# A graph attention layer on one core: TensorE copies the queries of four tiles to PSUM with identity products, VectorE multiplies and sums them there

## What is computed

```python
Q = (jnp.einsum('nc,rch->rnh', x, Wq) + bq[:, None, :]).reshape(R, N, HEADS, OUT)
K, V = ...                                   # the same with Wk, bk and Wv, bv
q_i = Q[edge_type, dst]
k_j = K[edge_type, src]
v_j = V[edge_type, src]
score = jnp.sum(q_i * k_j, axis=-1) * scale
seg = dst * R + edge_type
m = jax.ops.segment_max(score, seg, num_segments=N * R)
e = jnp.exp(score - m[seg])
s = jax.ops.segment_sum(e, seg, num_segments=N * R)
alpha = e / s[seg]
out = jax.ops.segment_sum(v_j * alpha[..., None], dst, num_segments=N)
x = _layernorm(x + out.reshape(N, HD) + bias, axis=-1)
```

## Time and profile before

| | us |
|---|---|
| median of three timed runs (lowest, highest) | 3232.29 (3231.82, 3235.07) |
| the profiled execution, its own time | 3212.14 |
| its span, first to last instruction | 3210.3 |
| busy: PE / VectorE / ScalarE / POOL | 1759.5 / 1668.4 / 1012.9 / 1763.2 |

### The profile page before, as it was taken

One profiled execution on the slowest core, in us unless ns is written; L12 is line 12 of the kernel. 1 busy time (PEld: TensorE's weight loads), 2 busy tenths in 40 slices (PEclk: granted clock), 3 DMA queues, 4 the chain that ended last, 5 costly groups with the idle time before them and its releaser, 6 DMA issues.

```text
span 3210.3 us, 25454 instructions
## 1 busy us (share of the span) xinstructions
PE 1759.5 (55%) x6003; PEld 1152.3 (36%) x6003; DVE 1668.4 (52%) x3077; ACT 1012.9 (32%) x3902; POOL 1763.2 (55%) x1794
## 2 busy tenths in 40 slices
PE   7999833333699952443444444444444444444479
PEld 3444311111244422343433333434433433333455
DVE  8884100000244346565656665656666656566666
ACT  2233200000000002444544454445445444444541
POOL 1004577666100027676777767777777777676435
PEclk9999955555899985566656656666666566656665
DMA  5335776676434457555656555655555565565413
GB/s 177 108 120 190 253 228 215 204 219 207 164 147 159 152 197 226 175 172 174 177 171 178 176 172 169 176 175 174 176 168 174 173 177 174 167 180 169 130 45 103
DMA packets 285615, 553.24 MB, mean 172 GB/s; under 512 B 43605, under 2 KB 167719, under 8 KB 285466
## 3 DMA queue, kind: packets, MB, share of 16 engines
q0 software_dynamic: 106496, 327.26, 35.2%
q1 hardware_dynamic: 142836, 156.41, 14.8%
q10 hardware_dynamic: 36134, 67.94, 5.8%
HBM read 397.78 MB, written 153.65 MB: 172 GB/s over the span
## 4 chain that ended last, share of the span: by engine, by line
PE 30%; another core or an unknown queue 23%; issue 17%; DVE 17%; ACT 10%; POOL 2%; DVEq 1%; DMA 1%; SPq 0%; ACTq 0%; POOLq 0%
PE sums L549 15%; ACT region L768 9%; PE sums L610 8%; DVE acc L1025 5%; DVE region L963 3%; POOL region L378 2%; DVE region L831 2%; PE sums L653 2%; PE sums L651 2%; DVE region L1012 2%; DVE region L965 2%; DVE region L942 1%; PE sums L546 1%; PE bank L570 1%
## 5 line engine op out<-in xcount | busy, mean ns | idle before, releaser
L610 PE MATMUL sums<-region 128*128 128x130 f32 x3328 | 754.2, 408 | 964.9 <-DVE region L1029 460.8
L378 POOL DMA_INDIRECT region<-kv_tab,kvidx x832 | 854.7, 1027 | 752.3 <-DVE region L956 352.7
L610 PEld LDWEIGHTS sums<-region 128*128 128x128 f32 x3328 | 692.8, 311 | 1017.2 <-issue 725.6
L549 PE MATMUL sums<-region,acc 128*128 128x512 f32 (+2 forms) x1568 | 759.7, 631 | 307.7 <-issue 174.3
L768 ACT ACTIVATE region<-region 128x64 f32<-128x64 f32 x3328 | 835.1, 334 | 102.1 <-issue 97.8
L1025 DVE TENSOR_TENSOR acc<-acc,sums 128x256 f32 x832 | 348.2, 419 | 544.3 <-remote 352.7
L361 POOL DMA_INDIRECT region<-q_tab,qidx x391 | 372.8, 953 | 438.1 <-DVE qidx L867 253.6
L549 PEld LDWEIGHTS sums<-region,acc 128*128 128x128 f32 (+1 forms) x1568 | 304.1, 205 | 687.5 <-issue 517.7
L942 DVE TENSOR_TENSOR region<-sums,region 128x512 f32<-128x512 f32 (+1 forms) x245 | 168.8, 691 | 698.8 <-remote 312.6
L383 POOL DMA_INDIRECT region<-q_tab,qidx x441 | 454.7, 1031 | 134.6 <-issue 134.6
L748 ACT COPY region<-bank 128x128 f32<-128x128 f32 x26 | 6.9, 266 | 1316.9 <-issue 988.2
(11 more groups left out here) (175 smaller groups left out, 873.1 us busy)
## 6 DMA issues: line engine op xcount, KB each, us to landing
kv_tab<-region ACTq DMA_DIRECT2D x48, 1280.0 KB
q_pre<-region SPq DMA_DIRECT2D x391, 128.0 KB
region<-q_pre SPq DMA_DIRECT2D x391, 128.0 KB
q_tab<-region SPq DMA_DIRECT2D x48, 640.0 KB
region<-q_tab,qidx POOLq DMA_INDIRECT x832
region<-kv_tab,kvidx POOLq DMA_INDIRECT x832
region<-in_x SPq DMA_DIRECT2D x96, 128.0 KB, 2.2
out<-region SPq DMA_DIRECT2D x48, 128.0 KB, 1.7
```

The costliest lines, as they stand in the source:

```text
L378: pool.indirect_dma_start(ring[:, s % KS, i, :], None, kv_tab, bass.IndirectOffsetOnAxis(ap=kvidx[:, t:t + 1], axis=0)).then_inc(s_got[s % ...
L549: done = nc.tensor.matmul(bank[o % 4][0:n, 0:w], acc[:, k, t * P:t * P + n], w_sb[:, k, :, :].rearrange("p u c -> p (u c)")[:, c0:c0 + w], ...
L610: done = nc.tensor.matmul(bank[i][:, h * W:(h + 1) * W], ring[:, q % KS, i, h * P:(h + 1) * P], oneh[:, q % 2, i, :], start=True, stop=True)
```

## The change

In each pass TensorE first runs a new function, `lift(s)`. It waits for the gathered rows of step s, its query rows and the scores of the step before, and multiplies the 128x1024 queries by the identity in two products of 128x512, which puts a copy in PSUM banks 4 and 5 (now one tensor, `pairs`). It raises a new semaphore, s_lift. VectorE waits for that one and for the gathered rows, multiplies the keys in SBUF with the queries in PSUM, writes over them in PSUM, and reduces from there. POOL and SP wait for s_lift where they waited for s_sc before they refill a slot of `qring`.

```diff
         bank = [sums[:, i, :] for i in range(4)]
-        bank += [ctx.enter_context(nc.psum_tensor(f"bank{i}", [P, 512], f32)) for i in range(4, 8)]
+        pairs = ctx.enter_context(nc.psum_tensor("pairs", [P, 2, 512], f32))
+        bank += [pairs[:, i, :] for i in range(2)]
+        bank += [ctx.enter_context(nc.psum_tensor(f"bank{i}", [P, 512], f32)) for i in (6, 7)]
+
+        qk = pairs.rearrange("p b (i w) -> p (b i) w", w=C)
...
                 if s >= QS:
-                    pool.wait_ge(s_sc, s - QS + 1)
+                    pool.wait_ge(s_lift, s - QS + 1)
...
                 if s >= QS:
-                    sp.wait_ge(s_sc, s - QS + 1)
+                    sp.wait_ge(s_lift, s - QS + 1)
...
+            def lift(s):
+
+                pe.wait_ge(s_got[s % KS], gathered(s))
+                pe.wait_ge(s_gotq[s % QS], 16 * sum(AHEAD[s % QS:s + 1:QS]))
+                if s > 0:
+                    pe.wait_ge(s_sc, s)
+                for half in range(2):
+                    done = nc.tensor.matmul(bank[4 + half][:, 0:2 * C], ident[:],
+                                            qring[:, s % QS, 2 * half:2 * half + 2, :].rearrange("p i c -> p (i c)"),
+                                            start=True, stop=True)
+                done.then_inc(s_lift, 1)
+
             pe.wait_ge(s_ready, 1)
             for s in range(NSB + LAG):
                 q = s - LAG + 1
+                if s < NSB:
+                    lift(s)
                 weights_a(s)
...
             def scores(s):
                 dve.wait_ge(s_got[s % KS], gathered(s))
-                dve.wait_ge(s_gotq[s % QS], 16 * sum(AHEAD[s % QS:s + 1:QS]))
-                q = qring[:, s % QS, :, :]
-                c(nc.vector.tensor_tensor(q, ring[:, s % KS, :, 0:C], q, ALU.mult))
+                dve.wait_ge(s_lift, s + 1)
+                c(nc.vector.tensor_tensor(qk, ring[:, s % KS, :, 0:C], qk, ALU.mult))
                 g = SB * (s % PERC)
                 nc.vector.tensor_reduce(sc[:, (s // PERC) % 2, :, g:g + SB].rearrange("p h g -> p g h"),
-                                        q.rearrange("p i (h d) -> p i h d", h=H), AX.X, ALU.add).then_inc(s_sc, 1)
+                                        qk.rearrange("p i (h d) -> p i h d", h=H), AX.X, ALU.add).then_inc(s_sc, 1)
```

More of the change, by code:

```diff
@@ L256, in gnn_kernel @@
         s_gotq = [sem(f"s_gotq{i}") for i in range(QS)]
-        s_sc = sem("s_sc")
+        s_lift, s_sc = sem("s_lifted"), sem("s_sc")
         s_ST, s_S, s_ends, s_rowT, s_row, s_cr, s_carT, s_car = (
```

## The result

| | kernel before | changed kernel | ratio (95% interval) |
|---|---|---|---|
| first comparison, 20 runs each | 3229.38 us | 3244.31 us | 1.0048 (1.0036 to 1.0060) |
| again (e18_again) | 3233.14 us | 3252.71 us | 1.0056 (1.0038 to 1.0074) |
| again, a chip on which the kernel before takes 17% less (e13_again) | 2664.08 us | 2615.75 us | 0.9824 (0.9807 to 0.9841) |

What follows compares the result with a forecast made beforehand. No engine is full; a chain of TensorE's aggregation and VectorE's accumulation, one-hot and scores bounds the edge stage. Lift +60 and POOL -10 give +50: 3232.3 + 50 = 3282 us; forecast's own range 3242 to 3362, whole range 3145 to 3365.

Steps and rivals of the forecast that it cites:

- my likeliest case: The forecast itself: the whole kernel gets slower, 3242 to 3362 us with 3282 as its value; chance 0.43.
- The lift, +60: Edge stage: TensorE's two added products per step delay VectorE's multiplication; between 0 and 168 us, taken as 60.
- short steps: Edge-stage steps of 5.27 to 5.62 us, three per chunk, where the lift would make VectorE's multiplication up to 2.15 us late.
- the sign: Before VectorE's multiplication: idle time grows from 23 us to 60 or more, with TensorE's lift as its releaser.
- the following long one: Long step after a short one: takes back part of the delay, as VectorE waits 3.8 and 4.5 us there anyway.
- TensorE's room: Edge stage: TensorE, busy 790 of 1863 us, can take 412 to 786 us more; only the lift's place matters.
- Multiplication and reduction in PSUM, 0: VectorE's score instructions: an operand in PSUM costs 2 ns per 512 elements, below 2 us for 416 instructions.
- POOL, -10: POOL's gathers, no longer delayed by the multiplication, save 81 ns each, 104 us in all; 10 us on the path.
- Slots, 0: Query slots refilled after the lift instead of the scores: worth 0, as no POOL wait names the scores.
- Rival A: Edge stage: POOL's gathers are the bound, so shorter gathers make the kernel faster, 3128 to 3180 us; chance 0.32.
- Rival B: Before VectorE's accumulation: late signals grow a quarter with TensorE's work, 88 us more, 3370 us in all; chance 0.12.
- C: Edge stage: short steps run at full clock or long steps give back all; 3232 us within 6; chance 0.13.

Runs made afterwards that it cites:

- e18_again: The changed kernel as it is, run again on a first-kind chip; 3252.71 us, 1.0056 against the kernel before.
- e13_again: The changed kernel as it is, run again on a chip where the kernel before takes 17% less; 2615.75 us, 0.9824 against the kernel before.
- e2_awaited: As e1_unused, but VectorE also waits for the lift before multiplying in SBUF; 3251.3 us, 1.0083 against the kernel before.
- e1_unused: The changed kernel with the lift made but not awaited or read, VectorE multiplying in SBUF; 3246.37 us, 1.0063 against the kernel before.
- e4_free: The kernel before plus two 128x512 identity products per step ahead of the aggregation, unread and not awaited; 3241.54 us, 1.0052.
- e3_port: The changed kernel with one lift, at step 0; every multiplication reads those queries from PSUM, so scores are wrong; 3217.97 us, 0.9979 against the kernel before.
- e7_slots: The changed kernel, but POOL and SP refill a query slot after the scores, not the lift; 3223.26 us, 1.0059 against the kernel before.
- e8_act4: The kernel before with one ScalarE scaling per tile instead of four, using the first head's weight only; 3190.07 us, 0.9964.
- e5_tiny: As e4_free, but the two free products have 2 columns instead of 512; 3223.85 us, 1.0057 against the kernel before.
- e6_double: As e4_free, but four free 128x512 products per step instead of two; 3257.55 us, 1.0163 against the kernel before.

## Why the prediction was right in sign and wrong in size

Right: slower by over 0.2%, my likeliest case at 0.43, and 3244 lies in the range of 3145 to 3365. Wrong: 15 us where 50 were forecast, and the result just reaches the lower end of the forecast's own range (3242).

**The lift, +60: this is the step that failed.** The sum of the lateness came near: I had 78 short steps late by up to 2.15 us, 131 us by the clock's share, and VectorE's idle time before the multiplication rose by 112 us. That is in part luck. Of the 135.4 us only 47.9 end with the lift, where I had named 60 or more as the sign; 66.3 us come from late signals, which I had not priced for the lift. There are 63 waits in all, 23 of them longer than 2.15 us, and the 78 was one chunk's count times 26, where the trace of the kernel before has 64 steps under 6.5 us. Wrong was "somewhat under half of that": I let 60 stay. The idle time before the next accumulations took all of it back (144 us less), as VectorE, coming later, waited less for signals that were late anyway; e2_awaited against e1_unused shows it with nothing else changed (138 us more at one wait, 126 less at the other, 5 us in the time). I had named this, but only for "the following long one", and set it at a half. The runs give the size of what stays: 17 to 21 us for the instructions alone (e4_free, e1_unused), some 5 more for waiting (e2_awaited), 22 to 26 in all against my 60. The lift by ScalarE supports the order of these two: without TensorE's instructions 14 us of it go.

**TensorE's room.** "It has the room, so the question is only where a lift lies on the chain" was wrong in its second half. The lift costs though nobody waits for it; it stands ahead of the aggregation and the softmax's transposes in TensorE's order. I had passed over the latter as waiting for VectorE's work, which comes later than the lift; the longer waits of the scan speak against it, without proving it. Nor does its price go with 1.98 to 3.78 us a pair: products of two columns cost the same.

**Multiplication and reduction in PSUM, 0:** right; 9 and 5 ns, 3 us in all. The earlier trace rows were enough.

**POOL, -10:** right; -8 measured alone (e3_port, -2 to -12 by its interval). The longest gathers did go (at most 1477 ns against 2492), though 81 ns a gather was the forecast and 61 and 56 ns came (the earlier trace rows against L382 and L387): the mean that is left is 966 and 975 ns, not the median of 947. The Trainium skill, "SBUF — State Buffer", Who interferes with whom, said that with one SBUF input there is no such contention. The half of it that no row had shown agrees with the runs: the mean fell to 956 to 976 ns in every run with one operand in PSUM, and stayed at 1024 to 1056 for the key and value gathers in those with two.

**Slots, 0:** right within the interval (e7_slots).

**The sum by the runs:** +0.63% for the lift unused, +0.20 for the wait, -0.21 for the gathers: +0.6%; measured +0.48 and +0.56.

**Rival A** (POOL's gathers are the bound, 3128 to 3180) was refuted on this chip by e3_port and is what happens on the other kind. My argument against it, that VectorE hardly waits for data, was sound: there VectorE waits 264 to 370 us for them or for a lift that waits for them. **Rival B** (late signals grow with TensorE's work, over 440 us) is refuted: 260.7 us after, 341 to 387 with free products. **C** (nothing left) is excluded by the interval.

**Not settled:** what makes the late signals on the first kind of chip. They don't come from ScalarE's many instructions (e8_act4) and don't grow in step with TensorE's work. They come on chips where the tables are written at some 210 GB/s and not where at 363: in e13_again every recorded increment by the aggregation between 850 and 2300 us, 724, stands within 15 ns of its product's end. Whether slower memory makes both wasn't tried.

Nor is it known how an added product that nobody waits for comes to cost time, why two short ones cost what two long ones do, and why four cost 1.6%, three times what two cost. One rival wasn't tried: more products are also more code to load. One instruction queue of the profile (q8) moves 49 packets of 16 KB in the kernel before, 55 with two free products, 62 with four and 49 with ScalarE's lift. Against it, the traces of the kernel before, of e5_tiny and of e6_double show no idle time of TensorE over 0.1 us, from 1250 to 3000 us, before a product that waits for nothing.

## What to carry to other kernels

Before pricing a delay on a chain that already holds waits, add up the waits behind it on the same engine: they can take back nearly all of it, as here. A product added ahead of a critical one can cost time even if it is short and nobody waits for it, so measure that price alone, with free products, before the rest; and try the work on an engine that arrives early, as ScalarE here, where it cost 14 to 17 us less. And an edit that trades one engine's time for another's changes its sign with the bound, so ask which wait ends last on each chip that the kernel is to run on.

## What the runs showed of the hardware

- The same kernel takes 3203 to 3233 us on some chips and 2664 to 2673 on others; the tables are written at 204 to 218 GB/s or at 363. The change is +0.5% on the first and -1.8% on the second.
- On the first kind TensorE's signals, and some of ScalarE's, come late without a visible cause, up to 12.4 us behind the product's modelled end; VectorE's come within 13 ns. On the second kind TensorE's come within 15 ns.
- Two products of 2 columns a step cost as much (1.0057) as two of 512 (1.0052), on two chips of the first kind.
- POOL's gathers of key and value rows take 1024 to 1056 ns in the mean beside multiplications with both operands in SBUF, 956 to 976 with one in PSUM.
- VectorE writes a result of 1024 elements to PSUM, and reduces 1024 from there, within 1% of the time in SBUF (1219 against 1210 ns, 1226 against 1221).
